# A GRU of 256 steps on one core: the second rest of chunk 1 of r*h moves from VectorE to GpSimd, and two products of gate R change places

## The reference

```python
ys = cond / sqrt(256);  d = rsqrt((ys*ys) @ (W0*W0) + 1e-8)
x1 = x + ((x * ys[:, None, :]) @ W0) * d[:, None, :]
def step(H, xs):                       # 256 times; H is (8, 256), H0 = cond
    Z = sigmoid(xz + H @ Whz.T + bhz)
    R = sigmoid(xr + H @ Whr.T + bhr)
    H_tilda = tanh(xh + R * H @ Whh.T + bhh)
    H_new = Z * H + (1.0 - Z) * H_tilda
    Y = H_new @ Whq.T + bhq
out = x1 + Y                           # xz, xr, xh = x1 @ Wx*.T + bx*
```

## Time and profile before

| | us |
|---|---|
| median of 3 runs (lowest, highest) | 636.63 (636.57, 637.08) |
| the profiled execution | 637.65 |
| its span, first to last instruction | 635.9 |
| TensorE busy in the span | 624.7 |
| VectorE busy | 465.4 |
| ScalarE busy | 279.5 |
| GpSimd busy | 4.5 |

### The profile page before, as it was taken

One profiled execution on the slowest core, in us unless ns is written; L12 is line 12 of the kernel. 1 busy time (PEld: TensorE's weight loads), 2 busy tenths in 40 slices (PEclk: granted clock), 3 DMA queues, 4 the chain that ended last, 5 costly groups with the idle time before them and its releaser, 6 DMA issues.

```text
span 635.9 us, 40091 instructions
## 1 busy us (share of the span) xinstructions
PE 624.7 (98%) x16890; PEld 566.6 (89%) x16890; DVE 465.4 (73%) x3794; ACT 279.5 (44%) x2119; POOL 4.5 (1%) x11
## 2 busy tenths in 40 slices
PE   8999999999999999999999999999999999999987
PEld 3589999999999999999999999999999999999976
DVE  3888777776777777777777777777677777767776
ACT  2244444444444444444444444444444444444443
POOL 0200000000000000000000000000000000000000
PEclk9955555555555555555555555555555555555555
DMA  7000000000000000000000000000000000000000
GB/s 265 2 4 4 5 12 5 3 13 4 13 4 13 4 5 12 5 12 5 11 6 4 13 4 13 4 5 12 5 12 5 12 5 4 12 4 13 4 12 12
DMA packets 7176, 8.87 MB, mean 14 GB/s; under 512 B 1618, under 2 KB 5458, under 8 KB 6996
## 3 DMA queue, kind: packets, MB, share of 16 engines
q1 hardware_dynamic: 6416, 6.03, 3.0%
q10 hardware_dynamic: 580, 0.28, 0.2%
HBM read 4.21 MB, written 2.10 MB: 10 GB/s over the span
## 4 chain that ended last, share of the span: by engine, by line
PE 93%; DVE 4%; ACT 1%; DMA 1%; issue 1%; DVEq 0%
PE chunk_bank L691 53%; PE z_rec_bank L691 13%; PE chunk_bank L668 12%; PE z_bank L668 6%; PE y_bank L653 6%; PE chunk_bank L700 2%; DMA x<-x_cm 1%; PE chunk_bank L605 1%; DVE lin L404 1%; DVE r_hidden L538 1%; DVE hidden L584 1%; DVE r_hidden L542 0%; DVE r_hidden L546 0%; ACT scan_mul L343 0%; DVE xs L397 0%
## 5 line engine op out<-in xcount | busy, mean ns | idle before, releaser
L691 PE MATMUL chunk_bank<-r_hidden,w_part 128*128 128x8 bf16 x6144 | 206.3, 169 | 0.2
L691 PEld LDWEIGHTS chunk_bank<-r_hidden,w_part 128*128 128x128 bf16 x6144 | 184.7, 105 | 19.5 <-issue 0.6
L343 ACT ACTIVATE scan_mul<-z_pre 128x16 f32<-128x16 f32 x256 | 57.2, 224 | 196.8 <-DVE z_pre L550 196.8
L691 PEld LDWEIGHTS chunk_bank<-hidden,w_part 128*128 128x128 bf16 x3072 | 102.8, 104 | 30.8 <-DVE hidden L584 6.0
L691 PE MATMUL chunk_bank<-hidden,w_part 128*128 128x8 bf16 x3072 | 125.2, 173 | 4.4 <-DVE hidden L584 3.9
L691 PE MATMUL z_rec_bank<-hidden_parts,w_part 128*128 128x24 bf16 x3072 | 121.6, 181 | 0.1
L691 PE MATMUL chunk_bank<-hidden_parts,w_part 128*128 128x8 bf16 x3072 | 117.8, 168 | 0.0
L538 DVE TENSOR_TENSOR r_hidden<-r_bank,hidden 128x8 f32<-128x8 f32 x256 | 42.6, 166 | 97.0 <-ACT r_bank L341 95.3
L691 PEld LDWEIGHTS z_rec_bank<-hidden_parts,w_part 128*128 128x128 bf16 x3072 | 103.3, 104 | 0.2 <-DVE z_rec_bank L486 0.2
L691 PEld LDWEIGHTS chunk_bank<-hidden_parts,w_part 128*128 128x128 bf16 x3072 | 101.5, 104 | 0.0
L584 DVE TENSOR_TENSOR_SCAN hidden<-scan_mul,r_bank 128x24 f32<-128x24 f32 x256 | 52.0, 203 | 58.0 <-ACT r_bank L346 52.2
(11 more groups left out here) (92 smaller groups left out, 801.5 us busy)
## 6 DMA issues: line engine op xcount, KB each, us to landing
x<-x_cm SPq DMA_DIRECT2D x4, 512.0 KB, 8.1
out_cm<-result SPq DMA_DIRECT2D x15, 128.0 KB, 2.2
w_rec<-w_rec_cm SPq DMA_DIRECT2D x1, 768.0 KB, 8.5
w_in<-w_in_cm SPq DMA_DIRECT2D x1, 768.0 KB, 10.2
w_mod<-w_mod_cm ACTq DMA_DIRECT2D x1, 256.0 KB, 5.7
w_out<-w_out_cm SPq DMA_DIRECT2D x1, 256.0 KB, 10.6
out_cm<-result SPq DMA_DIRECT2D x1, 64.0 KB, 2.5
out_cm<-result SPq DMA_DIRECT2D x2, 32.0 KB, 1.9
```

The source lines that it names most:

```text
L343: nc.scalar.activation(scan_mul[:, :, 2::3], z_pre[:, :, :], ACT.Sigmoid, scale=-1.0)
L691: return nc.tensor.matmul(cols, w_part[wp][:, gate, k, m * P:(m + 1) * P], moving, start=first, stop=True, skip_group_check=True)
```

## The change

GpSimd gets a loop over the 256 steps: it waits for the first rest of chunk 1 of r*h (rh_rest[1]) and computes the second rest of that chunk, with the same operands that VectorE had. VectorE keeps the second rest of chunk 0 and goes on to the sum of Z. TensorE waits for the same semaphore as before. In gate R, not in gate G, the two products (1, 0, 2, 1) move from ahead of the wait for the second rest of chunk 1 to behind the product that waited for it, which raises pre_r0.

```diff
@@ GpSimd, behind its set-up @@
+            for t in range(T):
+                pool.wait_ge(rh_rest[1], t + 1)
+                nc.gpsimd.tensor_tensor(r_hidden[:, 1, 2, :], r_hidden[:, 1, 1, :], rh_parts(1, 1, 2),
+                                        ALU.subtract).then_inc(rh_rest2[1], 1)
@@ VectorE, in each step @@
-                for k in range(KC):
-                    dve.wait_ge(rh_rest[k], t + 1)
-                    nc.vector.tensor_tensor(r_hidden[:, k, 2, :], r_hidden[:, k, 1, :], rh_parts(k, 1, 2),
-                                            ALU.subtract).then_inc(rh_rest2[k], 1)
+                dve.wait_ge(rh_rest[0], t + 1)
+                nc.vector.tensor_tensor(r_hidden[:, 0, 2, :], r_hidden[:, 0, 1, :], rh_parts(0, 1, 2),
+                                        ALU.subtract).then_inc(rh_rest2[0], 1)
@@ TensorE, gate_products @@
                 products(0, 0, 1, 2)
-                products(1, 0, 2, 1)
+                if gate == G:
+                    products(1, 0, 2, 1)
                 pe.wait_ge(rest2[1], t + 1)
                 products(0, 1, 1, 2).then_inc(done[0], 1)
+                if gate == R:
+                    products(1, 0, 2, 1)
                 products(1, 1, 2, 1)
```

## The result

The changed kernel takes 664.83 us (4 runs, 664.72 to 666.66) against 636.69 for the kernel before (4 runs); the ratio is 1.045, 95% interval 1.043 to 1.047. It is slower by 28.1 us. The forecast was 670 with a range of 640 to 700. The profiled execution took 664.80, its span is 663.0.

A forecast was written before the change was run, and what follows sets the result against it. Bound by a ring of waits run through once a step, TensorE waiting for operands. Gate R +0.05, GpSimd +0.09, Z sum -0.01: +0.13 a step, +33.3 us on 637.65, median 1.0 lower: 670 us, range 640 to 700.

The forecast's parts named there:

- The ring and its two tight places: Each step's waits form a ring; no slack at gate G's 20th load, and tanh bound by the Z sum by about 0.01.
- Gate R's swap, +0.05 a step: Gate R: load 18 waits for h's second rest, so chunk 1's first rest of r*h comes 0.05 us later.
- The gain of 0.01 for chunk 0: Gate R: product 20, which raises pre_r0, becomes product 18 and can start 0.01 us sooner, at 305.40.
- GpSimd, L = 0.29: End of chunk 1's first rest of r*h to end of its second: start 0.15 plus body 0.14 us on GpSimd.
- The Z sum, -0.01: VectorE's Z sum can come 0.10 us earlier; tanh, behind sigmoid Z, gains only 0.01 a step.
- The sum, +0.13 a step: Whole step: +0.05 gate R's stall, +0.09 GpSimd in place of VectorE, -0.01 Z sum; +33.3 us in all.
- The rival of the blocked GpSimd: In 80 steps VectorE's odd job blocks GpSimd's second rest for 0.27 us: 21.6 us on top, 691 us; chance 0.15.
- the odd job: VectorE operation of 0.28 us on two SBUF inputs after the Z sum in 80 steps, expected to start at 304.14.
- The time by the Trainium skill's figures: GpSimd's second rest: 60 ns fixed, 77 ns for 8 columns, L 0.23, about 655 us; the memset row was preferred.
- A reading: TensorE's granted clock was read as 0.5 of full speed in all slices of the steps, 1.2 GHz.

The follow-up runs named there:

- e6_swap_no_wait: Kernel before with gate R's two products moved, the 18th taking chunk 1's first rest of h so it needn't wait: 635.8 us, ratio 0.9994.
- e2_swap_alone: Kernel before, both second rests on VectorE, with only gate R's two products moved as in the change: 647.74 us, ratio 1.018.
- e1_gpsimd_alone: Changed kernel with gate R's products put back, so only the GpSimd part remains: 653.81 us, ratio 1.028.
- e7_vector_job128: Changed kernel plus one VectorE operation per step, two SBUF inputs of 128 columns, ahead of the Z sum: 681.61 us.

## Why the prediction was right

The place, the mechanism and the size held: 28.1 us slower, 33 forecast. One of its terms came out by luck. By its own steps:

- **The ring and its two tight places.** They hold. The 20th load of gate G follows its operand by 0.05 in every kernel here, and e6_swap_no_wait shows that chunk 1's side is the ring.
- **Gate R's swap, +0.05 a step.** e2_swap_alone: +0.044. The gain of 0.01 for chunk 0 was worth nothing, since chunk 0 doesn't bind (e6_swap_no_wait).
- **GpSimd, L = 0.29.** Measured 0.28, but from two errors that cancel, which is luck. The start I took as 0.15 after VectorE's end, from L286 in the set-up, is 0.08; that row had a second wait in it, which may be the difference. The body I put at 0.14, near the memset, is 0.20: a subtraction with two reads takes 0.09 more than the memset's 0.11, not 0.03. Had only one of the two been off, L would have been 0.22 or 0.35 and the time 652 or 685 us. The net cost of GpSimd for VectorE is 0.08, foreseen 0.09.
- **The Z sum, -0.01.** Tanh came 0.01 to 0.02 sooner (0.22 after load 20, it was 0.24, and 0.16 long instead of 0.17). GpSimd with the Z sum: +0.068 in e1_gpsimd_alone, foreseen +0.08.
- **The sum, +0.13 a step.** Measured +0.118 in the mean, +0.121 in the middle step. Of the 5 us by which 670 was too high, 3.3 are this (0.13 x 256 = 33.3, measured 30.0) and the rest is the set-up, which no step of the prediction had.
- **The rival of the blocked GpSimd.** The mechanism exists (e7_vector_job128) but not here: since GpSimd starts at 0.08, not at 0.15, it is there before the odd job. I had the two within 0.01 of each other; it was 0.05, on the good side. GpSimd's 256 operations all last 0.198 to 0.200, those beside an odd job too.
- **The time by the Trainium skill's figures.** The Trainium skill ("GPSIMD Engine Reference", section 3.1) led to a fixed part of 60 ns and to about 655 us; the operation lasts 198 ns, so the rows next to it were the better guide.
- **A reading.** The granted clock isn't 0.5 in all slices of the steps: the second slice of the earlier trace rows, up to 31.8 us, reads 9, and the steps start at about 26. It enters no term.

## What to carry to other kernels

When a step is a ring of short operations, an operation of the ring that moves to another engine costs the difference of the two paths from operand to user, semaphores included, times the steps, however idle the other engine is. Keep the operand that is awaited last on the quicker engine, and give the other one an operand that has slack, as much as its path is longer. Moving work out of the way of an awaited result earns next to nothing if the result's own operand isn't there sooner: compare the end of the operation that makes it with the start of the load that uses it. Before a reordering within a pair of chunks, find out which chunk's chain the ring runs through. And compare the steps apart from the set-up: here the set-up alone differs by up to 3 us between executions.

## What the runs showed of the hardware

- A two-input GpSimd subtraction of 128x8 float32 takes 0.198 us and starts 0.08 after the end of the VectorE operation that it waits for; VectorE takes 0.167 for the same and starts 0.03 after. The whole path is 0.28 against 0.20.
- A VectorE operation on two SBUF inputs that starts 0.08 us ahead of GpSimd's makes that one 0.06 longer with 128 columns (0.258 us) and not with 64 (0.200). The other way round, a VectorE operation of 128 columns that starts 0.05 behind GpSimd's is 0.016 longer, and one that starts 0.07 behind is not. Neither engine kept the other out for its whole length.
- The same eight float32 products after an idle TensorE took 3.67, 5.35 or 6.51 us, starting 0.43 us apart at a granted clock of 1.00 and 0.85 apart at 0.50. In some traces the first record of the clock begins only at 13 us, and a window ahead of it reads 1.00.
